# Attention over a graph: the denominators summed on GpSimd once per group instead of on TensorE every eight tiles

## The chip, the core and the metric

The kernel runs on one core of a Trainium2 chip. The metric is the time of one execution on the device in microseconds; before the change it was 7688.16 us, the median of three runs (7679.8 to 7697.36). The core has a matrix engine (TensorE, PE in the profile), VectorE (DVE), ScalarE (ACT), GpSimd (POOL) and SyncE (SP), which each run their own list of instructions and wait for each other on semaphores.

## The reference

A network of four graph layers over 6250 nodes with 64 features: two attention layers over 200,000 edges, a sum over neighbours, a dot-product attention over the edges, and two graph convolutions. The change touches the dot-product attention alone:

```python
scores = jnp.sum(qk[dst] * qk[src], axis=-1) / math.sqrt(v.shape[-1])
scores = jnp.clip(scores, -5.0, 5.0)
seg_max = jax.ops.segment_max(scores, dst, num_segments=n)
e = jnp.exp(scores - seg_max[dst])
seg_sum = jax.ops.segment_sum(e, dst, num_segments=n)
attn = e / seg_sum[dst]
out = jax.ops.segment_sum(attn[:, None] * v[src], dst, num_segments=n)
```

## The kernel before

The attention is computed densely. An earlier stage has counted how often each pair of nodes has an edge; the counts lie in DRAM as a bf16 matrix of 49 x 49 tiles of 128 x 128. The clipped exponential of a score, times the count, is the weight of a pair. For each node the kernel needs the sum of weights times values, and the sum of the weights (the denominator).

The 49 tiles of destination nodes are taken in groups of four (`GT`), twelve groups and a last one with a single tile. In a group the first 48 tiles of source nodes are taken two by two: 24 units (`UNITS`) of 128 x 1024 numbers (two source tiles by four destination tiles), and the 49th tile by itself at the end (`UNITS` as a unit number, `wt_end`, 128 x 512). In the last group a unit holds eight source tiles, so there are six (`FEW`).

For each unit:

- TensorE multiplies keys by the group's queries (`score`, L1986) into one of two PSUM buffers `sps`.
- ScalarE turns it into the exponential in `ex` (four slots): by `low` and `late` (L2109, L2113) in three units of four, by `direct` (L2099) in the fourth, and VectorE clips that one (`clip`, L2162).
- VectorE multiplies by the counts `adj` (the weighing, `weigh`, L2186 or L2183) into `wt` (six slots).
- TensorE multiplies values by the weights (`value`, L2001), four units (`LAG`) behind the score, and adds up in PSUM.
- After two units VectorE adds their weights (`join`, L2201) into `two` (four slots of 128 x 1024): twelve joins in a group.

The denominators are sums over the source nodes, which lie on the partitions; TensorE forms them as products with a matrix of ones (`total`, L2012). Every two joins, that is every eight source tiles, it takes four products of 512 columns, on the four column quarters of the array, and adds up in the PSUM bank `dps`. There are six `total` in a group, the last two in the first units of the next group, and `total_end` (L2025) for the 49th tile. At the end ScalarE copies both PSUM banks to SBUF (`evacuate`, L2093, L2094), TensorE turns them back to node rows (`turn_back`, L2034, L2035), and VectorE divides (`finish`, L2205 to L2209).

The order on each engine is written out by hand in the `group` functions, with semaphores between them. `s_sum` counts joins, `s_ones` the totals, and a join waits on `s_ones` until its slot of `two` has been read. GpSimd does nothing in this stage but clear semaphores at its start.

Of the kernel before, what the change touches and what calls it, by code (L numbers as in the profile page):

```python
# [1839 lines left out]
def attention(nc, k, adj_d, keys, values, out, ident, ones):  # L1840
# [18 lines left out]
    s_low, s_late, s_sum, s_ones = (k.sem("at_" + n) for n in ("low", "late", "sum", "ones"))  # L1859
    s_score, s_exp, s_clip, s_weight, s_value, s_evac, s_fold, s_out = (  # L1860
        k.sem("at_" + n) for n in ("score", "exp", "clipped", "weight", "value", "evac", "folded", "out"))
    with ExitStack() as own:
# [10 lines left out]
        two = k.sb("at_two", [P, TS, GT, 2, P], F32, own)  # L1873
        sums = k.sb("at_sums", [P, W], F32, own)
# [7 lines left out]

        @block.gpsimd
        def _(pool):
            clear_gone(pool, k)
# [41 lines left out]
        def ones_of(g, jj):  # L1927

            return g * (UNITS // 4 + 1) + (jj + 1 + AHEAD)

        def back(g, u, slots):

            return units_of(g, u - slots) if u >= slots else units_of(g, u + UNITS - slots - (UNITS + 1))

# [27 lines left out]
        def _(pe):  # L1962
# [42 lines left out]
            def total(g, jj, tiles):  # L2005
                w = tiles * P
                if jj == 0:
                    pe.wait_ge(s_evac, g + 2)
                if tiles == GT:
                    pe.wait_ge(s_sum, sums_of(g, 2 * jj + 1))  # L2010
                    for i in range(4):
                        last = pe.matmul(dps[32 * i:32 * i + 32, 0:w], ones[:, 0:32],  # L2012
                                         two[:, (2 * jj + i // 2) % TS, :, i % 2, :], start=(jj == 0), stop=False)
                else:
                    pe.wait_ge(s_sum, sums_of(g, jj))
                    for i in range(2 * GT):
                        last = pe.matmul(dps[32 * (i % 4):32 * (i % 4) + 32, 0:w], ones[:, 0:32],
                                         two[:, jj % TS, i // 2, i % 2, :], start=(jj == 0 and i < 4), stop=False)
                last.then_inc(s_ones, 1)

            def total_end(tiles):
                w = tiles * P
                for h in range(4):
                    at = slice(h * w // 4, (h + 1) * w // 4)
                    last = pe.matmul(dps[32 * h:32 * h + 32, at], ones[:, 0:32], wt_end[:, at], start=False, stop=True)  # L2025
                last.then_inc(s_ones, 1)

            def turn_back(g, tiles):
                pe.wait_ge(s_evac, g + 3)
                pe.wait_ge(s_out, g + 1)  # L2030
                pe.wait_ge(s_exp, directs_of(g, UNITS if tiles == GT else 4 * (FEW // 4)))
                for a in range(tiles):
                    at = slice(a * P, a * P + P)
                    pe.matmul(folded[:, a, 0:D], sums[:, at], fold[:], start=True, stop=True)  # L2034
                    last = pe.matmul(folded[:, a, D:D + 1], dens[:, at], pick[:], start=True, stop=True)  # L2035
                last.then_inc(s_fold, 1)
# [5 lines left out]
            def group(g, turn, tiles, odd, first=False):  # L2042
                pe.wait_ge(s_ask[odd], turn * 16 + 16)
                n = units_in(tiles)
                for u in range(n):
                    score(g, u, tiles, odd)
                    if u >= LAG:
                        value(g, u - LAG, tiles, odd)
                        if tiles == GT and (u - LAG) % 4 == 1 and u - LAG >= 5:
                            total(g, (u - LAG) // 4 - 1, tiles)  # L2050
                    elif not first:
                        value(g - 1, u + UNITS + 1 - LAG, GT, 1 - odd)
                        if u == 0:
                            total(g - 1, UNITS // 4 - 2, GT)
                        if u == LAG - 1:
                            total(g - 1, UNITS // 4 - 1, GT)
                            total_end(GT)
                    if u == (9 if tiles == GT else n - 1) and not first:
                        turn_back(g - 1, GT)
                score(g, UNITS, tiles, odd)  # L2060
                if tiles == GT:
                    value(g, UNITS - LAG, tiles, odd)
# [9 lines left out]
            for jj in range(FEW // 2):  # L2072
                total(GROUPS, jj, LAST)
            value(GROUPS, UNITS, LAST, 0)
            total_end(LAST)
# [4 lines left out]
        def _(act):  # L2080
# [5 lines left out]
            def evacuate(g, tiles, odd):  # L2086
# [3 lines left out]
                act.wait_ge(s_ones, ones_of(g, UNITS // 4 if tiles == GT else FEW // 2))  # L2090
# [3 lines left out]
                act.activation(dens[:, 0:w], dps[:, 0:w], ACT.Copy).then_inc(s_evac, 1)  # L2094
# [54 lines left out]
        def _(dve):  # L2149
# [38 lines left out]
            def weigh_end(g, tiles):  # L2188
# [3 lines left out]
                dve.wait_ge(s_ones, ones_of(g - 1, UNITS // 4))  # L2192
# [4 lines left out]
            def join(g, j):  # L2197
                dve.wait_ge(s_weight, units_of(g, 2 * j + 1))
                jj = j // 2
                dve.wait_ge(s_ones, ones_of(g, jj - 2) if j >= TS else ones_of(g, jj + UNITS // 4 - 2 - (UNITS // 4 + 1)))  # L2200
                dve.tensor_tensor(flat(two[:, j % TS]), flat(wt[:, 2 * j % WS]), flat(wt[:, (2 * j + 1) % WS]), ALU.add).then_inc(s_sum, 1)  # L2201
# [266 lines left out]
```

## Time and profile before

| | us |
|---|---|
| median of the runs | 7688.16 |
| the profiled execution, from outside | 7706.77 |
| its span, first to last instruction | 7704.8 |
| TensorE busy, products | 5782.3 |
| VectorE busy | 4089.8 |
| ScalarE busy | 2572.1 |
| GpSimd busy | 3042.2 |

Most of the span, some 5900 us, belongs to the two attention layers over the edges. The stage of the change runs from about 6428 to 7166, 738 us. The profile's views used below are: the busy time of each engine in a stretch (windows), the instructions in order of time (timeline; start, duration, engine, line, operation, and in brackets the idle time before it), the waits by who was waited for, and the durations of one line's instructions. Durations of neighbouring instructions of one engine overlap a little, so the distance from start to start tells what an instruction occupies. The timeline counts a TensorE product in f32 as two records.

### The profile page before, as it was taken

Reading aid. Unit: us, or ns where it says so; the run is one execution under the profiler, and the core shown is the slowest. Engines: PE = TensorE matmul, PEld = TensorE weight load, DVE = VectorE, ACT = ScalarE, POOL = GpSimd, SP = SyncE. Lnnn points to the kernel's source line nnn. Section 1 sums busy time; section 2 is a strip of 40 time slices with the busy share of each in tenths; the row PEclk is TensorE's granted clock in tenths of the full one; section 3 lists DMA queues with packets and bytes.
Section 4 is the critical chain, followed back from the end, with each engine's and each line's share of the span. In section 5 each row is a group of like instructions: output and inputs, shape, how many; then the busy total and the mean of one; then the engine's idle time right before and its main releaser. Section 6 shows DMA issues by size and latency. Waiting matters only on the chain. (4 is left out here: it accounts for less than half of the span.)

```text
span 7704.8 us, 170425 instructions
## 1 busy us (share of the span) xinstructions
PE 5782.3 (75%) x40520; PEld 4186.0 (54%) x40521; DVE 4089.8 (53%) x12731; ACT 2572.1 (33%) x4831; POOL 3042.2 (39%) x3157
## 2 busy tenths in 40 slices
PE   3777777777777776577777777777777698999699
PEld 2555555555555554455555555555555683222689
DVE  6455555555455555555555555555555527778532
ACT  2233333333333332333333323333333205777210
POOL 3555555555555553455555555555555000000000
PEclk9888888888888887788888888888888898999899
DMA  3333222232232332332332332332332362323479
GB/s 83 73 77 75 69 77 70 75 77 69 75 77 71 79 77 49 76 82 70 77 78 69 78 77 70 80 76 69 79 79 64 148 270 76 134 105 109 172 295 362
DMA packets 689323, 764.63 MB, mean 99 GB/s; under 512 B 368995, under 2 KB 574026, under 8 KB 664145
## 3 DMA queue, kind: packets, MB, share of 16 engines
q1 hardware_dynamic: 561781, 577.66, 24.5%
q0 software_dynamic: 100352, 102.96, 6.9%
q10 hardware_dynamic: 27102, 82.91, 2.8%
q8 instruction: 46, 0.75, 0.0%
q14 instruction: 42, 0.34, 0.0%
HBM read 671.04 MB, written 88.81 MB: 99 GB/s over the span
## 5 line engine op out<-in xcount | busy, mean ns | idle before, releaser
L336 POOL DMA_INDIRECT gat_rows<-rows_scr,gat_idx x3136 | 3015.6, 962 | 2862.7 <-PE gat_aps L1299 1237.0
L1290 PE MATMUL gat_tps<-ident,gat_weights 128*128 128x128 f32 x3136 | 601.2, 322 | 1319.3 <-ACTq L1155 1193.1
L1290 PEld LDWEIGHTS gat_tps<-ident,gat_weights 128*128 128x128 f32 x3136 | 384.1, 159 | 1508.1 <-ACTq L1155 1324.3
L1172 ACT ACTIVATE adj_tiles<-gat_counts 128x392 f32 (+1 forms) x784 | 390.8, 498 | 2161.2 <-remote 1135.1
L1308 PE MATMUL gat_sps<-gat_relu,gat_att 128*128 128x256 f32 x3136 | 1079.9, 478 | 0.0
L1071 DVE CUSTOM_DVE_ANT_0 gat_masked<-gat_sps,gat_miss,gat_oldtop 128x512 f32<-128x512 f32 x784 | 586.9, 749 | 754.6 <-remote 462.5
L1022 DVE TENSOR_SCALAR adj_hot_key<-adj_iota_key,adj_winbase,adj_key 128x392 bf16<-128x392 int16 x2416 | 960.5, 398 | 8.7 <-issue 8.7
L1299 PE MATMUL gat_aps<-gat_rows,gat_weightsT 128*128 128x65 f32 x6224 | 955.7, 306 | 0.0
L1299 PEld LDWEIGHTS gat_aps<-gat_rows,gat_weightsT 128*128 128x128 f32 x6224 | 938.5, 231 | 0.0
L1063 DVE COPY gat_oldtop<-gat_top 128x1 f32 x784 | 119.6, 153 | 1334.7 <-issue 622.2
L1021 DVE TENSOR_SCALAR adj_hot_lo<-adj_iota_lo,adj_low 128x128 bf16<-128x128 int16 x2416 | 636.9, 264 | 266.5 <-issue 108.4
L1308 PEld LDWEIGHTS gat_sps<-gat_relu,gat_att 128*128 128x128 f32 x3136 | 670.4, 237 | 73.0
L1161 ACT ACTIVATE gat_relu<-gat_mps 128x256 f32<-128x256 f32 x784 | 300.6, 383 | 1200.3 <-remote 1074.4
L1245 PE MATMUL gat_counts<-adj_hot_key,adj_hot_lo 128*128 128x392 bf16 x2416 | 640.0, 376 | 66.6 <-DVE adj_hot_key L1022 50.8
L1275 PE MATMUL gat_mps<-gat_ea,gat_we 128*128 128x256 f32 x1568 | 534.0, 425 | 178.8 <-DVE gat_miss L1056 77.1
L1151 ACT ACTIVATE gat_weights<-gat_masked,gat_newtop 128x512 f32<-128x512 f32 x788 | 565.6, 718 | 166.3 <-DVE gat_newtop L1071 107.0
L1166 ACT ACTIVATE gat_weightsT<-gat_tps 128x512 f32<-128x512 f32 x788 | 469.0, 595 | 380.6 <-remote 199.6
L1282 PE MATMUL gat_mps<-ident,gat_rows 128*64 128x128 f32 x6272 | 519.7, 280 | 8.0 <-issue 5.0
L1275 PEld LDWEIGHTS gat_mps<-gat_ea,gat_we 128*128 128x128 f32 x1568 | 311.5, 216 | 292.2 <-issue 258.7
L1485 PE MATMUL gcn_sum_b<-gcn_parts,gcn_sum_adj 128*128 128x193 bf16 x4802 | 414.9, 249 | 70.2 <-ACT gcn_parts L1504 70.2
L1245 PEld LDWEIGHTS gat_counts<-adj_hot_key,adj_hot_lo 128*128 128x128 bf16 x2416 | 271.7, 113 | 334.1 <-issue 120.1
L1485 PEld LDWEIGHTS gcn_sum_b<-gcn_parts,gcn_sum_adj 128*128 128x128 bf16 x4802 | 414.0, 98 | 70.9 <-issue 70.4
(379 smaller groups left out, 6837.8 us busy)
## 6 DMA issues: line engine op xcount, KB each, us to landing
gcn_sum_adj<-adj_scr SPq DMA_DIRECT2D x98, 1568.0 KB, 8.5
gat_dstb<-dst_scr SPq DMA_DIRECT2D x784, 128.0 KB
gat_ea<-in_ea SPq DMA_DIRECT2D x784, 128.0 KB
gin_sum_adj<-adj_scr SPq DMA_DIRECT2D x49, 1568.0 KB, 8.5
adj_scr<-adj_tiles ACTq DMA_DIRECT2D x48, 1568.0 KB
at_adj<-adj_scr SPq DMA_DIRECT2D x60, 1024.0 KB, 9.5
gat_rows<-rows_scr,gat_idx POOLq DMA_INDIRECT x3136
gat_xr<-xr_scr SPq DMA_DIRECT2D x1568, 24.0 KB
```

The costliest lines, as they stand in the source:

```text
L336: pool.indirect_dma_start(ring.rows[:, u, c, 0:ROW], None, rows_d, bass.IndirectOffsetOnAxis(ap=ring.idx[:, u, c:c + 1], axis=0)).then_inc ...
L1021: dve.tensor_scalar(plan.hot_lo[:, slot, :], plan.iota_lo[:], plan.low[:, bass.ds(c, 1)], None, ALU.is_equal)
L1022: dve.tensor_scalar(plan.hot_key[:, slot, :], plan.iota_key[:], plan.winbase[:, bass.ds(w, 1)], plan.key[:, bass.ds(c, 1)], ALU.add, ALU.i ...
L1071: dve.tensor_tensor_reduce(masked[:, j, :], sps[j][:], miss[:, o, :], 1.0, oldtop[:, o:o + 1], ALU.add, ALU.min, accum_out=newtop[:, j:j + ...
L1151: act.activation(wts[:, j, :], masked[:, j, :], ACT.Exp, bias=newtop[:, j:j + 1], scale=-1.0)
L1245: return pe.matmul(bank[:, 0:WD * NT], plan.hot_lo[:, slot, :], plan.hot_key[:, slot, :], start=start, stop=False)
L1275: pe.matmul(mps[j][:, 0:GE // 2], we[:], ea[:, v, :], start=True, stop=False)
L1282: last = pe.matmul(mps[j][64 * (c // 2):64 * (c // 2) + 64, P * (c % 2):P * (c % 2) + P], rows[:, v, c, 0:D], ident[:], start=False, stop= ...
L1290: last = pe.transpose(tps[:, c * P:(c + 1) * P], wts[:, j, c * P:(c + 1) * P], ident[:])
L1299: last = pe.matmul(aps[:, 0:D + 1], wtsT[:, j, c * P:(c + 1) * P], rows[:, v, c, 0:D + 1].rearrange("p a f -> p (a f)"), start=(c == 0), s ...
L1308: last = pe.matmul(sps[j][:, h * (GE // 2):(h + 1) * (GE // 2)], att[:, h, :], relu[:, j, :], start=True, stop=True)
L1485: last = pe.matmul(banks[b % 2][:, 0:W], adj[:, b, hi * P:(hi + 1) * P], parts[:, hi, :], start=(hi == 0), stop=(hi == NT - 1))
```

## The change

VectorE's joins stay. GpSimd now adds joins 1, 2, ... of a group to join 0, each time over the whole 128 x 1024, into a new buffer `heap` with two slots for alternate groups. Each addition waits for the join (`s_sum`) and for the addition before it (`s_added`), the first of a group also until TensorE has read the slot of `heap` two groups back. That makes 11 additions in each of the twelve groups and 2 in the last. TensorE forms the sum over the partitions once: `total` waits for the group's last addition, takes two products of 512 columns from `heap` on two column quarters, and two of 256 from `wt_end`. Consequently `dps` is used on 64 partitions instead of 128 by the evacuation and the turn-back. A join that reuses a slot of `two` now waits for GpSimd's addition (`s_added`) instead of TensorE's total. The helper functions only move up, ahead of GpSimd's block.

```diff
+        heap = k.sb("at_heap", [P, 2, GT, 2, P], F32, own)
...
         @block.gpsimd
         def _(pool):
             clear_gone(pool, k)
+            pool.sem_inc(s_added, AHEAD)
+
+            def add(g, joins):
+                flat = lambda unit: unit.rearrange("p a h d -> p (a h d)")
+                to = flat(heap[:, g % 2])
+                pool.wait_ge(s_ones, ones_of(g - 2))
+                for j in range(1, joins):
+                    pool.wait_ge(s_sum, sums_of(g, j))
+                    if j > 1:
+                        pool.wait_ge(s_added, added_of(g, j - 1))
+                    pool.tensor_tensor(to, flat(two[:, 0]) if j == 1 else to, flat(two[:, j % TS]), ALU.add).then_inc(s_added, 1)
+
+            for g in range(GROUPS):
+                add(g, UNITS // 2)
+            add(GROUPS, FEW // 2)
...
-            def total(g, jj, tiles):
+            def total(g, odd, tiles):
                 w = tiles * P
-                if jj == 0:
-                    pe.wait_ge(s_evac, g + 2)
-                if tiles == GT:
-                    pe.wait_ge(s_sum, sums_of(g, 2 * jj + 1))
-                    for i in range(4):
-                        last = pe.matmul(dps[32 * i:32 * i + 32, 0:w], ones[:, 0:32],
-                                         two[:, (2 * jj + i // 2) % TS, :, i % 2, :], start=(jj == 0), stop=False)
...
+                pe.wait_ge(s_evac, g + 2)
+                pe.wait_ge(s_added, added_of(g, units_in(tiles) // 2 - 1))
+                for q in range(1 if tiles == GT else GT):
+                    for h in range(2):
+                        at = slice(0, GT) if tiles == GT else slice(q, q + 1)
+                        pe.matmul(dps[32 * h:32 * h + 32, 0:w], ones[:, 0:32], heap[:, odd, at, h, :], start=(q == 0), stop=False)
+                for h in range(2):
+                    at = slice(h * w // 2, (h + 1) * w // 2)
                     last = pe.matmul(dps[32 * h:32 * h + 32, at], ones[:, 0:32], wt_end[:, at], start=False, stop=True)
                 last.then_inc(s_ones, 1)
...
                     if u >= LAG:
                         value(g, u - LAG, tiles, odd)
-                        if tiles == GT and (u - LAG) % 4 == 1 and u - LAG >= 5:
-                            total(g, (u - LAG) // 4 - 1, tiles)
                     elif not first:
                         value(g - 1, u + UNITS + 1 - LAG, GT, 1 - odd)
-                        if u == 0:
-                            total(g - 1, UNITS // 4 - 2, GT)
                         if u == LAG - 1:
-                            total(g - 1, UNITS // 4 - 1, GT)
-                            total_end(GT)
+                            total(g - 1, 1 - odd, GT)
...
-                act.activation(dens[:, 0:w], dps[:, 0:w], ACT.Copy).then_inc(s_evac, 1)
+                act.activation(dens[0:D, 0:w], dps[0:D, 0:w], ACT.Copy).then_inc(s_evac, 1)
...
             def join(g, j):
                 dve.wait_ge(s_weight, units_of(g, 2 * j + 1))
-                jj = j // 2
-                dve.wait_ge(s_ones, ones_of(g, jj - 2) if j >= TS else ones_of(g, jj + UNITS // 4 - 2 - (UNITS // 4 + 1)))
+                dve.wait_ge(s_added, added_of(g, j - TS) if j >= TS else added_of(g - 1, j + UNITS // 2 - TS))
```

On TensorE, at the fourth unit of a group, where the group before is closed, before the change (`at_s` is `sps`, `at_v` the PSUM bank of values times weights, `at_d` is `dps`; ISA and REGISTER_ALU rows are waits and their registers):

```order
L1983 REGISTER_ALU
L1986 MATMUL at_s<-at_ask,keys 128x512 x2
L1994 REGISTER_ALU
L1998 MATMUL at_v<-at_wt_end,values 64x256 x2
L2010 REGISTER_ALU
L2012 MATMUL at_d<-at_two,ones 32x512 x4
L2025 MATMUL at_d<-at_wt_end,ones 32x128 x4
```

The same place after the change, up to the next score:

```order
L2003 REGISTER_ALU
L2006 MATMUL at_s<-at_ask,keys 128x512 x2
L2014 REGISTER_ALU
L2018 MATMUL at_v<-at_wt_end,values 64x256 x2
L2027 REGISTER_ALU
L2028 ISA
L2032 MATMUL at_d<-at_heap,ones 32x512 x2
L2035 MATMUL at_d<-at_wt_end,ones 32x256 x2
```

The place is the same, the products are fewer, and there is one wait more (L2028), the one for GpSimd's last addition. The five other `total` of a group, which stood behind a `value`, are gone.

On GpSimd, from the entry of the attention stage to its end, before and after (the difference as a whole is 26 rows, of which the first groups stand here):

```order
-L1883 UNCONDITIONAL_BRANCH
+L1936 UNCONDITIONAL_BRANCH
 L87 ISA x8
+L1949 TENSOR_TENSOR at_heap<-at_two 128x1024
+L1949 TENSOR_TENSOR at_heap<-at_heap,at_two 128x1024 x10
+L1949 TENSOR_TENSOR at_heap<-at_two 128x1024
+L1949 TENSOR_TENSOR at_heap<-at_heap,at_two 128x1024 x10
```

Where GpSimd had only cleared semaphores, each group now has eleven additions in a row, each behind waits of its own. VectorE's order of weighings, clips and joins is the same as before.

## Rows read from the trace of the kernel before

**Rows 1.** Windows, one whole group: stretch, length, busy of each engine, PEclk, DMA.
```profile
6721.84:6781.19 59.35, 59.35 (x273) 15.53 (x271) 47.48 (x48) 45.65 (x46) 0.00 (x0) 1.00 0.31 113
```

**Rows 2.** Timeline, TensorE's products: start, duration (us), line, operation.
```profile
6706.42 1.08 PE L2001 MATMUL at_v<-at_wt,values 128*64 128x512 f32 x4
...
6707.43 1.07 PE L2012 MATMUL at_d<-at_two,ones 128*32 128x512 f32 x8
...
6708.43 1.13 PE L1986 MATMUL at_s<-at_ask,keys 64*128 64x512 f32 x4
...
6732.16 0.65 PE L1998 MATMUL at_v<-at_wt_end,values 128*64 128x256 f32 x4
...
6732.74 1.06 PE L2012 MATMUL at_d<-at_two,ones 128*32 128x512 f32 x8
...
6733.95 1.13 PE L1986 MATMUL at_s<-at_ask,keys 64*128 64x512 f32 x4
```

**Rows 3.** Waits in the same group: us in total, times, longest.
```profile
ACT at_ex L2109 <- PE at_s L1986: 13.6, 11, 2.8
DVE at_wt L2186 <- ACT at_ex L2113: 11.7, 12, 2.6
```

**Rows 4.** Timeline of VectorE in the stage.
```profile
6742.79 0.69 DVE L2162 TENSOR_SCALAR at_ex<-at_ex 128x1024 f32<-128x1024 f32 x1
6743.43 1.23 DVE L2186 SCALAR_TENSOR_TENSOR at_wt<-at_ex,at_adj 128x1024 f32<-128x1024 f32 x1
6744.57 1.22 DVE L2201 TENSOR_TENSOR at_two<-at_wt 128x1024 f32<-128x1024 f32 x1
...
6767.25 0.15 DVE L2205 TENSOR_SCALAR at_den<-at_f 128x4 f32<-128x4 f32 x1
...
6768.20 1.22 DVE L2186 SCALAR_TENSOR_TENSOR at_wt<-at_ex,at_adj 128x1024 f32<-128x1024 f32 x1
...
6785.79 0.42 DVE L2167 TENSOR_SCALAR at_ex_end<-at_ex_end 128x512 f32<-128x512 f32 x1
...
6787.26 0.68 DVE L2194 TENSOR_TENSOR at_wt_end<-at_ex_end,at_adj 128x512 f32<-128x512 f32 x1
```

**Rows 5.** GpSimd's subtractions in the prologue: min/median/max ns, first and last start.
```profile
L603 POOL TENSOR_TENSOR g_sb<-gat_acc,adj_tiles x2: 3212/3922/4632, 77.3 to 80.5; 128x1600 f32<-128x1600 f32 x1, 128x1536 f32<-128x1536 f32 x1
L603 POOL TENSOR_TENSOR g_sb<-g_sb,adj_tiles x2: 3088/3151/3214, 103.7 to 106.8; 128x1600 f32<-128x1600 f32 x1, 128x1536 f32<-128x1536 f32 x1
```

**Rows 6.** Timeline of VectorE and GpSimd in the prologue.
```profile
77.34 7.80 POOL L603 TENSOR_TENSOR g_sb<-gat_acc,adj_tiles 128x1600 f32<-128x1600 f32 x2 [70.54 <-ACT adj_tiles L520]
...
77.51 4.69 DVE L737 SCALAR_TENSOR_TENSOR pro_cond<-pro_ranges,pro_whi,pro_junk 128x1564 f32<-128x1564 f32 x1
...
82.33 4.46 DVE L739 CUSTOM_DVE_ANT_0 pro_junk<-pro_cond,pro_dst_i 128x1564 f32<-128x1564 f32 x1
...
89.90 1.85 DVE L737 SCALAR_TENSOR_TENSOR pro_cond<-pro_ranges,pro_whi,pro_junk 128x1564 f32<-128x1564 f32 x1
...
103.61 7.98 DVE L737 SCALAR_TENSOR_TENSOR pro_cond<-pro_ranges,pro_whi,pro_junk 128x1564 f32<-128x1564 f32 x1
103.68 6.25 POOL L603 TENSOR_TENSOR g_sb<-g_sb,adj_tiles 128x1600 f32<-128x1600 f32 x2
```

**Rows 7.** Timeline of VectorE and GpSimd in the batch norm.
```profile
6347.29 6.99 POOL L1745 TENSOR_TENSOR bn_both<-x_sb,h_sb 128x3136 f32<-128x3136 f32 x1 [377.54 <-SPq L1677]
...
6352.53 1.83 DVE L1702 TENSOR_TENSOR bn_sums<-bn_sums,z_sb 106x64 f32<-106x64 f32 x1
```

**Rows 8.** Timeline, the last join of the last group.
```profile
7159.53 1.21 DVE L2201 TENSOR_TENSOR at_two<-at_wt 128x1024 f32<-128x1024 f32 x1
```

**Rows 9.** Windows, 200 us of an attention layer over the edges, columns as in 1.
```profile
1000.00:1200.00 200.00, 145.58 (x950) 108.64 (x948) 100.98 (x378) 61.18 (x133) 101.69 (x107) 0.83 0.27 68
```

## Prediction before the run

> **What bounds the kernel now.** I read the attention stage in four steps. First the windows view of one whole group, from the end score of one group to that of the next [rows 1]: 59.35 us, TensorE busy in all of it at a granted clock of 1.00, VectorE 47.48, ScalarE 45.65, GpSimd 0.00. Then the timeline of TensorE [rows 2]: products follow each other without a gap, so TensorE sets the pace. Then the waits of that group [rows 3]: VectorE waits 11.7 us for ScalarE, which itself waits 13.6 for TensorE; this is spare time, not a bound. Last, the timeline of VectorE [rows 4], to see what each of its operations occupies when they stand back to back. The stage holds twelve such groups and a short last one, so a change of 1 us in a group is 12 us of the kernel.
>
> **TensorE: what goes.** A `total` takes from 6707.43 to 6708.43, 1.00 us, for four products of 512 columns in four column quarters at once [rows 2]. There are six in a group. The last one with `total_end` takes from 6732.74 to 6733.95, 1.21 us. Removed: 5 x 1.00 + 1.21 = 6.2 us. Added: two products of 512 columns on two column quarters. The nearest row is `value`, two products of 512 columns on two halves, from 6706.42 to 6707.43, 1.01 us; and two of 256 columns, nearest the end value from 6732.16 to 6732.74, 0.58 us. Sum 1.6 us. The smaller evacuation and turn-back products (64 partitions for 128) change no column count and I cost them at nothing. TensorE would need 59.35 - 6.2 + 1.6 = 54.7 us for a group. If nothing else came late, the kernel would win 12 x 4.6 = 55 us.
>
> **VectorE: unchanged work.** The group has 24 weighings and 12 joins of 1024 columns, 1.14 us apart when nothing is waited for (6743.43 to 6744.57), 6 clips at 0.64 (6742.79 to 6743.43), `finish` at 0.95 (6767.25 to 6768.20), and the end clip and end weighing, 0.42 and 0.68, together about 1.0 in line [rows 4]. 36 x 1.14 + 6 x 0.64 + 0.95 + 1.0 = 46.8 us. This agrees with 59.35 less the 11.7 of waiting, 47.6. Alone that fits under 54.7 with 7.9 us to spare.
>
> **GpSimd: 11 additions a group, 134 in all.** The nearest row is `bn_both`, an addition of two f32 tensors of 3136 columns in 6.99 us, or 2.23 ns a column [rows 7]: 2.28 us for 1024 columns. The subtraction of an f32 and a bf16 tensor took 3.09 to 3.21 us for 1536 and 1600 columns when it was undisturbed [rows 5], 2.01 ns a column: 2.06 us, the lower bound. 11 x 2.28 = 25 us of a 54.7 us group: as a queue of its own GpSimd keeps up easily.
>
> **What speaks against it: the two engines do not run these operations side by side.** The trace shows it three times. (a) GpSimd started two subtractions at 77.34; together they took 7.80 us [rows 6], the first 3.21, the second 4.63 [rows 5]. VectorE's operation with two SBUF inputs that began at 77.51 took 4.69 us where a later one took 1.85, and ended at 82.20, which is 1.65 after the first subtraction's end at 80.55. The second subtraction then ended at 85.14, 2.94 after 82.20, and VectorE's next two-input operation ended at 86.79, 1.65 after that [rows 6]. Each ran while the other stood still. (b) VectorE's operation of 103.61 lasted 7.98 us and ended 1.66 after both subtractions of 103.68 were through (109.93) [rows 6]. (c) A VectorE addition of only 64 columns took 1.83 us and ended at 6354.36, 0.08 after `bn_both` ended at 6354.28 [rows 7]. So the instruction that finds the other engine inside one waits until it is over, and work of the two engines adds up. Weighings and joins all have two SBUF inputs. No row shows a clip against GpSimd; if clips were free of it, they could hide at most 6 x 0.64 = 3.8 us of GpSimd's time a group, which lies within my range.
>
> **The sum for the likeliest case.** VectorE and GpSimd together become the bound. An addition that waited for VectorE hides some of its start (2.94 after release for 3.09 alone), so I take 2.2 us for 2.28, near the f32 row because both inputs are f32: 11 x 2.2 = 24.2 us. `finish` reads PSUM and small tiles, and an addition is due just then, so its 0.95 us lies beside GpSimd. At the group's edge one bubble is new: the single `total` waits for addition 11; from its end TensorE needs 1.6 for the totals, then score 4, value 0 and score 5 at about 1.03 each, then ScalarE 1.1 for the evacuation and 1.14 for the exponential, with 0.3 for signals 7.2 us, while VectorE has work for 5 x 1.14 + 0.64 = 6.3. That is 0.9 us of waiting (bounds 0 and 1.6). A group: 46.8 - 0.95 + 24.2 + 0.9 = 71.0 us for 59.35, or 11.65 more; twelve of them 140 us. In the last group the last join begins at 7159.53 [rows 8]; an addition of 2.28 now stands between it and the totals, less some 1.2 us of saved small products, and one more addition falls among its weighings: 3 us. Together +143 us. The profiled execution took 7706.77 us, so 7850 for it; the median of the runs is 7688.16, 18.6 below, and 7688 + 143 = 7831.
>
> **Bounds.** Low: additions at 1.95 (2.06 less 0.1), no bubble: 45.85 + 21.5 = 67.3, +7.95 a group, 95 in all, 7783. High: 2.45 for an addition (2.28 and some 0.1 at each of two handovers), a bubble of 1.6, `finish` not hidden: 46.8 + 27.0 + 1.6 = 75.4, +16 a group, 192 and 5 for the end, 7885.
>
> **Rivals.** *The two engines overlap after all* (ends on the faster side). Either the blocking seen in the prologue does not touch these operations, or only some: a weighing's second input is bf16, and no row shows exactly that form against GpSimd. If only joins and clips were blocked, VectorE would need 46.8 and about 6 us of waits, 53, still under TensorE's 54.7. The decisive point is 7.9 us a group: if the time that VectorE loses to the 25 us of additions stays below it, TensorE stays the bound and the kernel takes 7688 - 55 + 2 = 7635. For it: nothing in the trace but that difference in types. Against it: three cases out of three in which a two-input operation met a GpSimd operation with reads, two with different opcodes. 9 in 100. *Handovers cost more.* Each addition makes two handovers; at 0.3 us each, not seen in the rows (1.65 after release for 1564 columns, 1.85 alone, so a gain if anything), a group is 11 x 0.6 = 6.6 longer and the kernel 79 longer, 7910. 4 in 100. *TensorE's clock falls*, because it is now busy 54.7 of 71 us. In an attention layer over the edges TensorE was busy 145.58 of 200 us at a mean clock of 0.83 [rows 9]; 54.7 / 0.83 = 66 us, still under 71, so the same clock costs nothing here. Only a mean below 0.77 would make TensorE the bound; at 0.72 a group takes 76 us and the kernel 7888. 3 in 100.
>
> [...]
>
> **How the numbers follow.** Serial case 84 in 100, at 7831; overlap 9; costly handovers 4; clock 3. About 0.2% (15 us) is what a measurement of this kernel can tell from no change. Faster by more: 0.09; within: 0.01; slower: 0.90. The range runs from 7783, the low bound, to 7875, somewhat inside the high one, since that needs all high ends at once. It leaves out the overlap and the two dear rivals and little more, about 2 in 10.
>
> **What the profile after would show.** Right: a group of about 71 us with VectorE busy nearly all of it; the mean duration of weighings and joins risen from 1.22 to about 1.9, since a blocked instruction counts as running; GpSimd busy some 300 us or more with means above 2.28, its own blocking included; gaps between TensorE's products and a share of busy time near 77%. Wrong: weighings still at 1.22 us beside running additions and groups of 55 us (overlap); additions of well under 2 us (the low end); weighings ending more than 1.2 us after an addition's end (handovers); a granted clock below 0.8 in the stage.

## The result and the profile after

The changed kernel takes 7854.42 us in the median (7835.02 to 7894.27), the kernel before 7690.36; the ratio is 1.0221, 95% interval 1.0176 to 1.0266. It is slower by 164 us. The forecast was 7831 with a range of 7783 to 7875. The profiled execution took 7841.02 us, 134 more than the 7706.77 of the one before.

One whole group, from end score to end score, is now 71.65 us long, for 59.35 in [rows 1]. Windows view (stretch, length, busy of PE, PEld, DVE, ACT, POOL, PEclk, DMA):

```profile
6754.50:6826.15 71.65, 59.49 (x224) 15.72 (x223) 69.08 (x48) 46.10 (x47) 35.41 (x11) 0.95 0.26 93
```

VectorE has gone from 47.48 us of busy time to 69.08 with the same 48 instructions, and TensorE is no longer busy all the time. Where VectorE's time went is in its groups by line for this stretch, after (busy us, mean ns, idle before):

```profile
L2189 DVE SCALAR_TENSOR_TENSOR at_wt<-at_ex,at_adj 128x1024 f32<-128x1024 f32 x19 | 35.0, 1847 | 2.3 <-ACT at_ex L2116 2.3
L2165 DVE TENSOR_SCALAR at_ex<-at_ex 128x1024 f32<-128x1024 f32 x6 | 14.9, 2486 | 0.0
L2203 DVE TENSOR_TENSOR at_two<-at_wt 128x1024 f32<-128x1024 f32 x12 | 14.6, 1212 | 0.0
L2170 DVE TENSOR_SCALAR at_ex_end<-at_ex_end 128x512 f32<-128x512 f32 x1 | 2.6, 2591 | 0.0
```

and for the group of [rows 1] in the kernel before:

```profile
L2186 DVE SCALAR_TENSOR_TENSOR at_wt<-at_ex,at_adj 128x1024 f32<-128x1024 f32 x19 | 23.3, 1224 | 12.3 <-ACT at_ex L2113 11.7
L2162 DVE TENSOR_SCALAR at_ex<-at_ex 128x1024 f32<-128x1024 f32 x6 | 4.1, 686 | 0.0
```

Weighings took 11.7 us more, clips 10.8, the end clip 2.2; joins are unchanged. (These rows count an instruction at the window's edge whole, and neighbours overlap a little, so their sum of 24.7 is more than the 21.6 us by which the busy time grew.) In exchange the wait for ScalarE shrank from 11.7 us [rows 3] to 2.3. The timelines of GpSimd and VectorE show why it is these:

```profile
6799.12 3.28 POOL L1949 TENSOR_TENSOR at_heap<-at_heap,at_two 128x1024 f32<-128x1024 f32 x1 [2.90 <-DVE at_two L2203]
6800.10 3.38 DVE L2189 SCALAR_TENSOR_TENSOR at_wt<-at_ex,at_adj 128x1024 f32<-128x1024 f32 x1
...
6803.41 1.21 DVE L2203 TENSOR_TENSOR at_two<-at_wt 128x1024 f32<-128x1024 f32 x1
...
6804.54 1.21 DVE L2189 SCALAR_TENSOR_TENSOR at_wt<-at_ex,at_adj 128x1024 f32<-128x1024 f32 x1
...
6804.70 3.27 POOL L1949 TENSOR_TENSOR at_heap<-at_heap,at_two 128x1024 f32<-128x1024 f32 x1 [2.29 <-DVE at_two L2203]
6805.68 2.85 DVE L2165 TENSOR_SCALAR at_ex<-at_ex 128x1024 f32<-128x1024 f32 x1
```

The join of 6803.41 ends and starts both the next weighing (6804.54) and the addition (6804.70). The weighing is first and runs its 1.21 us to 6805.75; the addition works from there to 6807.97, 2.22 us, though its row says 3.27. The clip was issued at 6805.68 and ends at 6808.53, 0.56 after the addition. Clip alone: 0.69. After the other join of a pair the same happens to a weighing, 3.38 for 1.22. So in a regular group each addition stops the second instruction behind its join, which is never a join, and makes it 2.17 us longer. In one place it is different, where `finish` stands behind the join:

```profile
6810.87 3.28 POOL L1949 TENSOR_TENSOR at_heap<-at_heap,at_two 128x1024 f32<-128x1024 f32 x1 [2.90 <-DVE at_two L2203]
...
6812.44 0.42 DVE L2211 TENSOR_TENSOR z_sb<-at_f,at_den 128x256 f32 x1 [0.18 <-issue]
6812.78 2.46 DVE L2189 SCALAR_TENSOR_TENSOR at_wt<-at_ex,at_adj 128x1024 f32<-128x1024 f32 x1
```

The addition works from the end of the weighing before it, 6811.93, to 6814.15. The last instruction of `finish` lies inside that time and takes 0.42 us as in the kernel before; only the weighing behind it is held, and for 1.25 us instead of 2.17. `finish` lies beside GpSimd, as forecast.

The group's edge is the other place where TensorE and VectorE stand. TensorE's timeline:

```profile
6839.70 0.65 PE L2018 MATMUL at_v<-at_wt_end,values 128*64 128x256 f32 x4 [2.10 <-DVE at_wt_end L2197]
6841.90 1.59 PE L2032 MATMUL at_d<-at_heap,ones 128*32 128x512 f32 x4 [1.55 <-POOL at_heap L1949]
6843.28 1.07 PE L2035 MATMUL at_d<-at_wt_end,ones 128*32 128x256 f32 x4
6844.28 1.81 PE L2006 MATMUL at_s<-at_ask,keys 64*128 64x512 f32 x4
6846.02 1.08 PE L2021 MATMUL at_v<-at_wt,values 128*64 128x512 f32 x4
```

The total waits 1.55 us for the eleventh addition, as forecast, but totals and score then take 4.12 us, where 2.63 were expected. The windows view shows the granted clock in that stretch:

```profile
6840.00:6844.00 4.00, 2.45 (x12) 0.52 (x8) 4.00 (x3) 0.00 (x0) 1.85 (x1) 0.78 1.05 388
6844.00:6847.00 3.00, 3.00 (x10) 0.70 (x8) 3.00 (x5) 0.86 (x1) 0.00 (x0) 0.72 0.89 329
```

The granted clock is 0.78 and 0.72 there, so for a part of each stretch it is 1.2 instead of 2.4 GHz, after TensorE had stood for 2.10 and 1.55 us. A second such stretch lies some 20 us ahead of the edge, 0.66 from 6821 to 6826. In the kernel before the granted clock was 1.00 in the whole group [rows 1].

From the first weighing to the first product of the stage behind it is 886.6 us (6413.03 to 7299.6), for 729.6 before (6436.59 to 7166.2): 157 us. Eleven distances between end scores account for 135 (71.64 for 59.34 each), the start of the stage for 7, its end for 15. The rest of that execution happened to be some 23 us shorter than in the one before.

### The profile page after: what moved, and what is told of

Its sections match the earlier page's. It is cut to its first block and busy times, and to the rows that moved or that the text cites. A ratio compares the mean times of both kernels' runs of the same rounds, so it can differ in the third digit from the quotient of the medians.

```text
span 7839.2 us, 169420 instructions
## 1 busy us (share of the span) xinstructions
PE 5771.6 (74%) x39908; PEld 4185.6 (53%) x39909; DVE 4348.4 (55%) x12731; ACT 2578.1 (33%) x4831; POOL 3489.9 (45%) x3291
## 5 line engine op out<-in xcount | busy, mean ns | idle before, releaser
L1949 POOL TENSOR_TENSOR at_heap<-at_heap,at_two 128x1024 f32<-128x1024 f32 x121 | 388.6, 3211 | 296.5 <-DVE at_two L2203 296.1
```

## The experiments

Two theories. *Exclusion*: an addition on GpSimd and most instructions of VectorE exclude each other, so that the price is the length of the addition. *Waits*: the changed order, the single total behind the last addition or the joins that wait for GpSimd, makes the loss. The runs were made on several chips; on two of them (e1 to e5, e7, e8 and a0) all of the kernel but this stage is faster and the kernel before takes 5934 and 5935 us. The length of a group is therefore what I compare; it is the distance from the first to the twelfth end score, divided by eleven, and reads the same on both kinds of chip (71.64 and 71.74 for the changed kernel). Of e1, e6 and a0 there are several executions, of each other experiment a single one, so its whole time is rough.

| kernel | a group, us | whole, us | before on the same chip |
|---|---|---|---|
| before | 59.34 | 7690.36 | |
| changed | 71.64 | 7854.42 | 7690.36 |
| a0, changed again | 71.74 | 6097.10 | 5935.17 |
| e1, no additions | 55.88 | 5893.12 | 5934.40 |
| e2, half additions | 58.47 | 5919.84 | 5934.40 |
| e3, fill for addition | 55.88 | 5890.00 | 5934.40 |
| e4, before and additions | 69.55 | 6050.33 | 5934.40 |
| e5, filler products | 70.56, the last seven 69.8 to 70.0 | 6093.92 | 5935.17 |
| e6, pairs on VectorE | 56.35 | 7673.54 | 7705.77 |
| e7, additions on VectorE | 62.57, five of 60.5 | 5986.91 | 5935.17 |
| e8, total later | 70.35, shortest 69.5 | 6071.03 | 5935.17 |
| e9, long fill | 55.89 | 7665.62 | 7705.77 |
| e10, pairs on GpSimd | 60.96, eight of 59.2 | 7738.16 | 7705.77 |

**The additions taken away, TensorE's part kept.**

```diff
-                    pool.tensor_tensor(to, flat(two[:, 0]) if j == 1 else to, flat(two[:, j % TS]), ALU.add).then_inc(s_added, 1)
+                    pool.sem_inc(s_added, 1)
```

> The changed kernel without GpSimd's additions: GpSimd fills both slots of heap once and afterwards only raises the semaphore when a join is there, so the denominators are wrong. All else, TensorE's fewer products too, is as in the changed kernel. Theory (VectorE and GpSimd exclude each other, and nothing else of the change costs): TensorE is the bound again, a group takes 54.7 us (59.35 before, 71.64 changed), weighings have a mean of 1.22 us, the kernel is about 55 us faster than before, some 7635. Rival (the new waits and the single total at the group's edge cost by themselves): a group stays above 60 us.

A group is 55.88 us, and the ratio to before is 0.9927 (0.9901 to 0.9953), 41 us faster. Two neighbouring groups in the windows view:

```profile
4761.30:4816.60 55.30, 55.30 (x225) 15.16 (x223) 47.03 (x48) 45.38 (x46) 0.00 (x0) 1.00 0.34 122
4816.60:4873.50 56.90, 56.90 (x224) 15.45 (x222) 47.10 (x48) 45.44 (x46) 0.00 (x0) 0.97 0.33 117
```

TensorE is the bound again, and all waits on semaphores are still there; so they don't make the loss. Groups are 55.3 us at a clock of 1.00, 0.6 more than the forecast sum, and 56.9 where the clock dips. The TensorE part of the change is worth 3.5 us a group, not 4.6.

The 0.6 us come from the turn-back. Its first product in the kernel before, and in e1:

```profile
6747.36 0.43 PE L2034 MATMUL at_f<-at_fold,at_sums 128*128 128x64 f32 x2
```

```profile
4785.04 0.44 PE L2045 MATMUL at_f<-at_fold,at_sums 128*128 128x64 f32 x2
```

From there to the next value product it is 2.93 us before (to 6750.29) and 3.66 here (to 4788.70), 0.73 more. The denominators' product has 64 partitions instead of 128 there; the forecast had put that at nothing. The totals take 1.42 us (4771.21 to 4772.63) for 1.6 in the sum.

**Half the columns.** The additions, in all kernels that have them, are those of the change except for what is named; here they cover columns 0 to 511.

```diff
+                    half = slice(0, GT * P)
+                    pool.tensor_tensor(to[:, half], flat(two[:, 0])[:, half] if j == 1 else to[:, half], flat(two[:, j % TS])[:, half], ALU.add).then_inc(s_added, 1)
```

> The changed kernel with additions of 512 columns instead of 1024, so half of each denominator is missing. Theory (the exclusion lasts as long as the addition): an addition holds VectorE up for about 1.1 us instead of 2.2, a group takes 71.6 - 11 x 1.1 = 59.5 us, near the time before. Rival (the price is one of handovers, by count): a group stays within 2 us of 71.6. Rival (blocking in whole turns of something else, such as the weighing before it): between the two, 65.

58.47 us, for 59.5 expected. The clips give the price: a stopped one takes 1.76 us for 0.68 alone, 1.08 more, where an addition of full length makes it 2.17 more. The price goes by columns, not by handovers. Dividing the group by 11 gives 1.06 too ((58.47 - 46.8) / 11), but that is chance: VectorE is busy in only 55.6 of 58.3 us of a group here, and some additions fall into its pauses. The durations of this kernel's clips and additions (min/median/max ns):

```profile
L2169 DVE TENSOR_SCALAR at_ex<-at_ex x73: 679/1755/1770, 4658.1 to 5358.9; 128x1024 f32<-128x1024 f32 x73
L1953 POOL TENSOR_TENSOR at_heap<-at_heap,at_two x121: 1264/2186/2197, 4669.9 to 5370.8; 128x512 f32<-128x512 f32 x121
```

**The kernel before, with additions on top that nobody waits for.**

```diff
+            other = keys[:, 0:8, :].rearrange("p t n -> p (t n)")
+            made = 0
+            for g in range(GROUPS):
+                for j in range(1, UNITS // 2):
+                    pool.wait_ge(s_sum, g * (UNITS // 2) + j + 1)
...
+                    pool.tensor_tensor(heap[:], heap[:] if made else other, other, ALU.add).then_inc(s_added, 1)
+                    made += 1
```

> The kernel before, with TensorE's totals untouched, and 11 additions of 1024 f32 columns a group on GpSimd on data of its own (the keys), each started by a join, their result used by nobody; nobody waits for GpSimd. Theory: the additions alone make the loss, VectorE and GpSimd serial again, 46.8 + 24 = 71 us a group (70 to 72.5), weighings and clips with maxima of about 3.4 and 2.8 us. Rival (the loss comes from joins or totals that wait for GpSimd): 59.35 as before.

69.55 us, from 59.34, with TensorE's list untouched and other tiles read by GpSimd. So it isn't a matter of the tiles either. It is a little below the 70 to 72.5 expected. (69.55 - 46.8) / 11 = 2.07 us for an addition in the mean; a stopped clip is 2.17 us longer, and the one addition of a group beside `finish` costs less. Its rows, and a group in the windows view:

```profile
L2172 DVE TENSOR_SCALAR at_ex<-at_ex x73: 679/2853/2864, 4660.1 to 5494.3; 128x1024 f32<-128x1024 f32 x73
L1894 POOL TENSOR_TENSOR at_heap<-at_heap,keys x131: 2737/3278/7276, 4672.5 to 5489.4; 128x1024 f32<-128x1024 f32 x131
4779.20:4849.00 69.80, 61.85 (x273) 15.94 (x271) 69.10 (x48) 45.98 (x47) 35.53 (x12) 0.98 0.27 96
```

VectorE is busy 69.10 of 69.80 us, as in the changed kernel. The changed kernel's remaining 2.1 us belong to its edge.

**Filling instead of adding.** First a fill as large as an addition, then, because it turned out to last only 0.95 us and to be over before a clip comes, a fill of 2048 columns.

```diff
-                    pool.tensor_tensor(to, flat(two[:, 0]) if j == 1 else to, flat(two[:, j % TS]), ALU.add).then_inc(s_added, 1)
+                    pool.memset(to, 1.0).then_inc(s_added, 1)
```

> The changed kernel with a fill of 1024 columns in place of each addition: GpSimd writes as much and reads nothing, so the denominators are wrong. Theory (what excludes is a read path that a second SBUF input of VectorE and GpSimd share): weighings and joins keep a mean of about 1.22 us, a group is near 55 us, at most 58 if clips still wait. Rival (any GpSimd instruction of this length blocks VectorE): weighings stretch by the length of the fill, a group over 62.

> The changed kernel with a fill of 2048 columns of a scratch tile in place of each addition (about 1.9 us, reads nothing), so that every fill started by the first join of a pair still runs when the clip that follows comes; the denominators are wrong. Theory (a clip runs at twice a weighing's pace and so takes GpSimd's write path as well): clips have a median of about 1.4 us, from 0.69, weighings stay at 1.22, and the group stays under 57. Rival (only GpSimd's reads exclude): clips stay at 0.69, as all others. Rival (a long fill blocks weighings too): weighings stretch to 2 or 3 us and the group goes beyond 60.

In e9 each fill goes to a scratch tile. Groups of 55.88 and 55.89 us, the same as without GpSimd. In the first, no instruction of VectorE is stretched. In the second (min/median/max ns):

```profile
L2166 DVE TENSOR_SCALAR at_ex<-at_ex x73: 678/1349/1510, 6438.1 to 7102.9; 128x1024 f32<-128x1024 f32 x73
L2190 DVE SCALAR_TENSOR_TENSOR at_wt<-at_ex,at_adj x221: 1204/1215/1227, 6434.9 to 7112.6; 128x1024 f32<-128x1024 f32 x111
L1950 POOL MEMSET at_junk<- x134: 1804/1804/1812, 6444.9 to 7115.9; 128x2048 f32 x134
```

Weighings run beside a fill of 1.80 us untouched, with 1.23 us at most; clips are held, 1.35 for 0.69, and such a clip ends 0.55 us after the fill, so it waits for the whole of it. Clips run at almost two columns in the time that a weighing takes for one. So two things stop VectorE: an instruction with two SBUF inputs stands against GpSimd's reads, a fast clip against its writes (and, in e4, against additions, which read and write; no run has a GpSimd instruction that reads alone).

**TensorE kept busy at the edge.**

```diff
+                pe.matmul(dps[:, 0:P], k.ones[:], k.ident[:], start=True, stop=True)
+                pe.matmul(dps[:, 0:P], k.ones[:], k.ident[:], start=True, stop=True)
                 pe.wait_ge(s_added, added_of(g, units_in(tiles) // 2 - 1))
...
+                    if tiles == GT and u >= 12:
+                        if u == 12 and not first:
+                            pe.wait_ge(s_evac, g + 2)
+                        fill(pe, k, dps, 3)
...
+                        fill(pe, k, dps, 3)
                         value(g - 1, u + UNITS + 1 - LAG, GT, 1 - odd)
```

> The changed kernel with three products of 128 columns more on TensorE per unit in units 12 to 23 and 0 to 3, and two before the wait for the last addition, into the bank of the denominators while it is free; TensorE has that much less idle time and the work is without use. Theory (a falling clock at the group's edge stretches the two totals and the next scores): the granted clock stays at 1.00 and a group shortens from 71.6 to about 70.2. Rival (the clock plays no part): 71.6 or, as the fillers stand in the way, more.

The first four groups were 71.4 to 72.3 us long, the seven after them 69.8 to 70.0. One of these:

```profile
5095.00:5165.00 70.00, 69.89 (x325) 27.60 (x323) 69.07 (x48) 46.08 (x46) 35.39 (x11) 1.00 0.26 96
```

The clock is 1.00 and VectorE's busy time is unchanged at 69.07; what went is its wait. TensorE's timeline shows where. Totals and score:

```profile
5109.20 1.05 PE L2034 MATMUL at_d<-at_heap,ones 128*32 128x512 f32 x4
...
5111.67 1.08 PE L2021 MATMUL at_v<-at_wt,values 128*64 128x512 f32 x4
```

They take 2.47 us for 4.12 in the changed kernel, and that is what a group has become shorter by: the lower clock at the edge is worth some 1.6 us a group. The edge is as short in the second group (4825.07 to 4827.55), which takes 71.6 all the same. There the clock falls elsewhere, behind the turn-back and where no filler stands:

```profile
4842.90:4846.90 4.00, 4.00 (x13) 1.00 (x12) 4.00 (x3) 2.71 (x3) 1.70 (x2) 0.67 0.00 0
```

Products of that kind, twice as long as the others, stand in the second to the fourth group at the same place and in no later one. Why the clock fell there and not later is open, and so is the length of the first group, 72.3 us at a clock of 1.00.

**The total two units later.**

```diff
-                        if u == LAG - 1:
-                            total(g - 1, 1 - odd, GT)
+                    if u == LAG + 1 and not first:
+                        total(g - 1, 1 - odd, GT)
```

> The changed kernel with the single total two units later, behind the sixth score and the second value of the next group, so that TensorE doesn't stand between the last addition and the fifth score. Theory (the edge of a group costs 2 us because fifth and sixth score wait for the total): a group shortens from 71.6 to 69.6, the serial sum of VectorE and GpSimd. Rival (the serial sum alone is 71.6): no change.

Expected were 69.6 us a group; five distances are 69.5 to 69.8, six are 70.9 to 71.0. One of each:

```profile
4711.30:4780.80 69.50, 57.78 (x224) 15.43 (x222) 68.74 (x48) 45.92 (x47) 34.54 (x12) 0.98 0.27 97
4850.30:4921.30 71.00, 60.73 (x224) 15.64 (x222) 69.97 (x48) 46.86 (x47) 34.79 (x12) 0.93 0.26 94
```

Without the total in its way the short group is the serial sum, as e4 has it, so the place of the total makes the edge dear. In this long one the granted clock is 0.93, but the group behind it takes 69.6 us at 0.92 (4921.3 to 4990.9), so the mean clock doesn't tell short groups from long ones; what lengthens the six is open. The serial sum of 69.5 stays in all of them.

**The same additions on VectorE.** `add` is moved to VectorE's list word for word, one or two operations behind its join.

```diff
+                    if u:
+                        add(g, u // 2 - 1, slot)
                     weigh(g, u + 2, GT)
                     join(g, u // 2)
                     weigh(g, u + 3, GT)
+                    if u:
+                        add(g, u // 2, slot)
...
-            with dve.Fori(1, GROUPS) as g:
-                group(g)
+            with dve.Fori(0, GROUPS // 2 - 1) as i:
+                group(i * 2 + 1, 1)
+                group(i * 2 + 2, 0)
```

> The changed kernel with the same 11 additions a group made by VectorE, each one or two operations after its join; GpSimd does nothing, TensorE as in the changed kernel. Theory (an addition costs VectorE its own time, wherever it runs): 1.14 instead of about 2.1 us each, 46.8 + 12.5 = 59.3, with up to 1 us at the edge 60 us a group, within 10 us of the kernel before. Rival (waiting for its own results costs VectorE more): 62 or more.

Five groups take 60.5 us, as expected, two 62.0 and four 65.4, and the kernel is 52 us slower than before, not within 10 as expected. Of the additional time of a long one the waits and the timeline of VectorE tell:

```profile
DVE at_wt L2175 <- issue: 4.6, 1, 4.6
```

```profile
4856.93 1.21 DVE L2198 TENSOR_TENSOR at_heap<-at_heap,at_two 128x1024 f32<-128x1024 f32 x1
4862.72 2.36 DVE L2175 SCALAR_TENSOR_TENSOR at_wt<-at_ex,at_adj 128x1024 f32<-128x1024 f32 x2 [4.57 <-issue]
```

In that time the DMA engines move the next group's counts (6 loads issued from 4847.34, DMA share 1.05 until 4862). The wait isn't for them: the first load, the one that this weighing needs, had landed at 4852.33, and a short group has the same loads at the same distance. The whole stage has four such waits, 18.1 us together, one in each long group and none elsewhere. They stand where VectorE's loop jumps back, which by this edit holds two groups in a round, and in each of them one 8 KB packet of instructions is fetched, about 2.2 us after its start (4860.37 in this one). So VectorE most likely waited for its own instructions, behind loads that keep the DMA engines full. No run moved the loads or the loop, so this is argued, not shown; and it is a cost of how this run was written, not of the additions.

**A mixture that stays under TensorE.** Six additions instead of eleven, on sums of two joins, and three totals instead of six; on VectorE, and the same on GpSimd.

```diff
+            def pair(g, q):
+                m = q // 2
+                dve.wait_ge(s_sum, sums_of(g, 2 * q + 1))
+                dve.wait_ge(s_ones, ones_of(g, m - 1) if m else ones_of(g - 1, UNITS // 8 - 1))
+                dve.tensor_tensor(flat(pairs[:, q % 2]), flat(two[:, 2 * q % TS]), flat(two[:, (2 * q + 1) % TS]), ALU.add).then_inc(s_pair, 1)
...
-                        if tiles == GT and (u - LAG) % 4 == 1 and u - LAG >= 5:
-                            total(g, (u - LAG) // 4 - 1, tiles)
+                        if tiles == GT and u - LAG in (11, 19):
+                            total(g, (u - LAG) // 8 - 1, tiles)
```

> The kernel before, in which VectorE adds its joins two by two once more (six additions of 1024 columns a group) and TensorE takes four products of 512 columns from two such sums, three totals a group instead of six. GpSimd does nothing. Theory (TensorE stays the bound while VectorE's sum stays under its own): TensorE 59.34 - 3 x 1.00 = 56.35, VectorE 46.8 + 6 x 1.14 = 53.6, so 56.4 us a group and 36 us less than before in all. Rival (VectorE's waits for its own results, or the loads of the counts, come late): 59 us or more a group.

> The same as e6_vector_pairs, with the six additions on GpSimd instead of VectorE. Theory (an addition on GpSimd takes 2.1 us from VectorE): 46.8 + 6 x 2.1 = 59.4 us a group less what is hidden, 58.5 to 60, 2 to 3 us a group more than with VectorE doing them. Rival (at six additions a group they fit into VectorE's idle time, since TensorE needs 56.35): 56.4.

On VectorE 56.35 us a group, to the hundredth the sum. The kernel takes 7673.54 us for 7705.77 on the same chip, ratio 0.9962 (0.9942 to 0.9982): faster than both kernels of this case. One group:

```profile
6535.20:6591.60 56.40, 56.40 (x251) 15.05 (x247) 53.25 (x54) 45.47 (x46) 0.00 (x0) 1.00 0.33 119
```

On GpSimd eight of the eleven distances are 59.2, which is 46.8 + 6 x 2.07 = 59.2, and three are 67.4, 67.8 and 62.0. The cause of the one with 67.4 is in the timelines of GpSimd and VectorE:

```profile
6563.36 9.00 POOL L1945 TENSOR_TENSOR at_pairs<-at_two 128x1024 f32<-128x1024 f32 x1 [5.50 <-DVE at_two L2210]
...
6568.95 1.21 DVE L2193 TENSOR_TENSOR at_wt<-at_ex,at_adj 128x1024 f32<-128x1024 f32 x1
6580.99 1.23 DVE L2196 SCALAR_TENSOR_TENSOR at_wt<-at_ex,at_adj 128x1024 f32<-128x1024 f32 x1 [10.82 <-ACT at_ex L2123]
```

This addition took 9.00 us, and TensorE's total waited for it. No instruction of VectorE was stretched meanwhile, for here the exclusion fell the other way: VectorE's weighings, clip and join followed each other without a gap from before 6563.36 to 6570.16, and the addition ended 2.20 us after that, which is the time that an addition works. The first addition of the changed kernel is such a one, 12.34 us, and ended 2.2 us after VectorE's first pause; five additions of e4 are too, with 7.27 us. In e4, e10 and the changed kernel alike, additions end 2.2 us after the last weighing, join or clip that they let pass, with few exceptions of up to 2.9. Mostly that is the one which is running, and then the addition holds VectorE; why it sometimes lets four to nine more pass is open.

**The changed kernel once more.**

> The changed kernel once more, on the chip of these runs. Theory: the loss belongs to the attention stage and not to the rest, so it is the same in microseconds, +130 to +165, and a group takes 71.6 us, whatever the time of the rest of the kernel is on this chip. Rival (a part of the loss is TensorE's lower clock, which differs between chips): a group near 70 us where the clock stays at 1.00.

6097.10 us for 5935.17, ratio 1.0273 (1.0256 to 1.029), or +162 us. The loss is the same in microseconds on a chip where the rest of the kernel takes 1750 us less.

## Where the prediction was right and where it was off

- *TensorE sets the pace before* and *it would win if nothing else came late*: right; e1. The win was put at 4.6 us a group; it is 3.5, and 4.0 where the clock stays up. The term that was missing is the turn-back, costed at nothing because its columns don't change: it takes 0.73 us more.
- *VectorE and GpSimd add up*: right; e4 shows it alone, e2 that it goes by length. The price of an addition was put at 2.2 us; a stopped instruction is 2.17 us longer. The clip was left open between free and blocked; it is blocked, and six of the eleven additions of a group fall on a clip, the end clip included.
- *`finish` lies beside GpSimd*: right; its rows are undisturbed and the weighing behind it is held for 1.25 us instead of 2.17. This is why the mean over eleven additions is 2.07 and not 2.17; with 0.95 us of `finish` hidden, e4's group gives (69.55 - 45.85) / 11 = 2.15.
- *The bubble at the edge*: right in kind and place (e8), too small in size. Put at 0.9, it is 2.1 (71.64 less 69.55), and VectorE waits 2.3. The term lacked TensorE's clock: after waits of 2.10 and 1.55 us the totals and the score run 1.5 us longer, and with the clock held at 1.00 they take 2.47 us for the 2.63 of the forecast (e5). The rival on the clock looked at the mean over the group, 0.95, which indeed costs nothing while VectorE is the bound; it matters where TensorE is on the path, which is just at the edge.
- The errors partly cancel, which is luck: the eleven additions less `finish` came to 0.5 us less than forecast, the edge to 1.2 more. 71.0 was forecast and 71.64 came.
- *The end of the stage +3 us*: too little. One group's share and that end were 11.65 + 3; start and end together are 22. The end scores of the last two groups lie 25.8 us apart for 18.4, and twelve filler products behind the stage, which the next stage waits for, took 5.49 us for 2.92 at a granted clock of 0.66 in that window (7290 to 7300). These 7 us are one half of why +157 us for the stage was above the +143 of the sum; the other half is eleven times the 0.65 us by which a group is longer than forecast. That the median moved by +164, near the stage's +157, while the profiled execution moved by +134, is the scatter of the rest.
- *Weighings and joins stretch to 1.9 us*: half right. Weighings on line L2189 have a mean of 1.85, joins 1.21; clips, with 2.49, weren't named. An addition starts when a join has ended, so in a regular group it doesn't meet one; the one stretched join of the stage, 3.37 us, follows the addition of 12.34. TensorE's share of busy time is 83%, for 77% forecast.
- The rivals: overlap is excluded by e4; handovers by e2.

The Trainium skill, page SBUF — State Buffer, section "Who interferes with whom", has two rules that the runs bear out: an instruction of VectorE with two SBUF inputs contends with GpSimd's reads but not with its writes (e4 against e9), and one in a two-port mode contends with GpSimd as such (the clips of e9, 1.35 for 0.69 us). That the clips run in such a mode is taken from their pace, 0.64 us for 1024 columns where a weighing has 1.14; no run switches it off.

Going on costs nothing that the rows show: a blocked clip ends 0.56 us after the addition, and alone takes 0.69.

## What to carry to other kernels

GpSimd is idle in a stage, but work moved to it isn't free: an addition of two SBUF tensors stops VectorE's weighings, joins and clips for all of its length, here 2.17 us, nearly twice the 1.14 that VectorE would need for it. What doesn't collide, here `finish`, is worth placing beside it. Look in the trace of the kernel for any place where both already meet; three rows of the prologue and the batch norm told the outcome of this change. If VectorE has spare time, give it as many of the additions as keep its sum under the bound (six were a gain; eleven, 60.5 us a group for 59.34, a loss), and where TensorE is on the path behind a wait, price its products at the clock that the rows show there.

## What the runs showed of the hardware that was not expected

- A fill on GpSimd (writes alone) leaves instructions of VectorE with two SBUF inputs at 1.21 us but stretches the clips from 0.69 to 1.35.
- TensorE's granted clock falls to its lower level for some microseconds after waits of 2.10 and 1.55 us at the edge of a group (0.72 to 0.78 in windows of 3 and 4 us), although it is busy 83% of the group. With filler products at the edge it stayed at 1.00 there, but in three groups it fell 30 us later (0.67 in a window of 4 us), where products had stood without a gap; in the last groups it stayed up.
- Chips differ. The kernel before takes 5934 us on one and 7690 on another, with a mean granted clock of TensorE of 0.96 and 0.87, whether as cause or as consequence isn't known; the attention stage alone is alike on both, 71.74 and 71.64 us a group for the changed kernel.
- The exclusion can fall the other way too: single additions on GpSimd took 7.27, 9.00 and 12.34 us while VectorE's instructions, unstretched, followed each other without a gap, and ended 2.2 us after its first pause.
- Not everything on VectorE is stopped: the short instructions of `finish` (0.42 us for the longest) run beside an addition at their own length.
